# One more 384-column matmul per group, its product thrown away, in the three gather passes of a four-layer graph network

## The reference

```python
edge_index = jnp.stack([src, dst])
h = jnp.maximum(_layernorm(x, axis=-1), 0.0)
x = x + _L0_gnn_ref(h, edge_index, edge_type_9, 12500, ...)      # sum of messages by target, then a GRU cell
h = jnp.maximum(_layernorm(x, axis=-1), 0.0)
x = x + _L1_gnn_ref(h, edge_index, ...)                          # degree-scaled sum by target, matmul, norm
h = jnp.maximum(_layernorm(x, axis=-1), 0.0)
x = x + _L2_gnn_ref(h, ..., edge_index, edge_type_50)            # a matrix per relation, summed by source
h = jnp.maximum(_layernorm(x, axis=-1), 0.0)
x = x + _L3_gnn_ref(h, edge_attr_64, src, dst, ...)              # attention: softmax over each target's edges
return x
```

## Time and profile before

| | us |
|---|---|
| median of 3 runs | 12327.03 (12316.74 to 12334.25) |
| profiled execution, its own time | 12320.53 |
| its span in the trace | 12318.4 |
| layer 0 gather pass, from 303.8 to 2707 | 2403 |
| layer 1 gather pass, from 2757.6 to 5526 | 2768 |
| layer 2 message pass, from about 5550 to 8460 | 2900 |
| layer 3 soft pass, from 9216 to 11845 | 2629 |

### The profile page before, as it was taken

The page is one execution under the profiler, slowest core; times in us unless marked ns, Lnnn a source line. Parts: engine busy times, 40 slices in busy tenths (PEclk is TensorE's granted clock), DMA queues, the critical chain, the costliest instruction groups (busy, mean ns, idle before and its releaser), DMA issues. The chain is left out here.

```text
span 12318.4 us, 152974 instructions
## 1 busy us (share of the span) xinstructions
PE 8202.7 (67%) x36696; PEld 6310.6 (51%) x36696; DVE 5261.8 (43%) x13087; ACT 1875.0 (15%) x5050; POOL 7137.0 (58%) x6298
## 2 busy tenths in 40 slices
PE   0566767665565655668888888884037777777752
PEld 0455555543333333337777777773026666666641
DVE  4344444445555555552222222224424444444455
ACT  1011111111111111112222222221011111111110
POOL 0666666656555555547888888884025555555510
PEclk6555555555555555557777777776556666666655
DMA  3521121111111111114444444445512222222211
GB/s 115 208 58 56 56 58 56 56 56 53 56 56 56 56 56 56 55 54 62 56 56 55 56 56 55 56 56 107 147 53 61 60 60 59 61 59 60 60 50 33
DMA packets 891203, 798.37 MB, mean 65 GB/s; under 512 B 140837, under 2 KB 778381, under 8 KB 891132
## 3 DMA queue, kind: packets, MB, share of 16 engines
q0 software_dynamic: 376576, 415.18, 18.6%
q1 hardware_dynamic: 504956, 376.73, 9.9%
q10 hardware_dynamic: 9600, 5.66, 0.2%
HBM read 544.97 MB, written 252.04 MB: 65 GB/s over the span
## 5 line engine op out<-in xcount | busy, mean ns | idle before, releaser
L1424 POOL DMA_INDIRECT scat<-msg_out,msg_idx x1568 | 2419.2, 1543 | 497.8 <-issue 477.9
L1970 POOL DMA_INDIRECT soft_x<-proj,soft_slot x1568 | 1527.1, 974 | 1792.5 <-ACT soft_slot L1991 1319.3
L991 POOL DMA_INDIRECT L_rows<-H,L_slot x1568 | 1558.0, 994 | 1189.6 <-ACT L_slot L1006 718.9
L714 POOL DMA_INDIRECT L_rows<-H,L_slot x1568 | 1617.5, 1032 | 1059.3 <-ACT L_slot L725 600.7
L1515 PE MATMUL msg_ps_msg<-msg_hb,msg_lhs 128*128 128x128 f32 x6272 | 1599.9, 437 | 1.6 <-DVE msg_lhs L1488 1.6
L1515 PEld LDWEIGHTS msg_ps_msg<-msg_hb,msg_lhs 128*128 128x128 f32 x6272 | 1492.9, 328 | 188.9 <-issue 187.2
L1488 DVE SCALAR_TENSOR_TENSOR msg_lhs<-msg_dst_sp,msg_node,msg_ps_c 128x512 f32<-128x512 f32 x784 | 551.2, 745 | 2030.9 <-ACT msg_dst_sp L1444 2025.0
L1164 PE MATMUL L_ps_type<-L_id_rows,select 5*50 5x512 bf16 x392 | 241.1, 615 | 1027.6 <-DMA L_id_rows<-rows 546.5
L853 PE MATMUL L_sum<-L_onehot,L_rows 128*128 128x64 f32 x3136 | 714.3, 393 | 292.6 <-issue 190.6
L2037 PE MATMUL soft_ps_x<-edge_wT,soft_atT 128*128 128x256 f32 x1568 | 785.9, 600 | 99.2 <-issue 99.1
L853 PEld LDWEIGHTS L_sum<-L_onehot,L_rows 128*128 128x128 f32 x3136 | 653.1, 301 | 371.3 <-issue 269.0
(11 more groups left out here) (367 smaller groups left out, 12350.5 us busy)
## 6 DMA issues: line engine op xcount, KB each, us to landing
scat<-L_zeros SPq DMA_DIRECT2D x128, 408.0 KB
rel_parts<-scat SPq DMA_DIRECT2D x400, 128.0 KB, 2.6
L_rows<-H,L_slot POOLq DMA_INDIRECT x3136
msg_hb<-HB SPq DMA_DIRECT2D x392, 128.0 KB
soft_at_in<-in_edge_attr_dram SPq DMA_DIRECT2D x391, 128.0 KB
HB<-L_prod SPq DMA_DIRECT2D x49, 512.0 KB
scat<-msg_out,msg_idx POOLq DMA_INDIRECT x1568
soft_x<-proj,soft_slot POOLq DMA_INDIRECT x1568
```

Of the source, the lines that this page charges most:

```text
L714: pool.indirect_dma_start(rows[:, k, j, :], None, t["H0"], bass.IndirectOffsetOnAxis(ap=slot[:, k, j:j + 1], axis=0)).then_inc(gathered[k] ...
L991: pool.indirect_dma_start(rows[:, k, j, :], None, t["H1"], bass.IndirectOffsetOnAxis(ap=slot[:, k, j:j + 1], axis=0)).then_inc(gathered[k] ...
L1424: pool.indirect_dma_start(t["scat"][(k * J + j) % COPIES], bass.IndirectOffsetOnAxis(ap=idx[:, k, j:j + 1], axis=0), out[:, k, j, :], None ...
L1970: pool.indirect_dma_start(x[:, s, j, :], None, t["proj"], bass.IndirectOffsetOnAxis(ap=slot[:, s, j:j + 1], axis=0)).then_inc(gathered[s % ...
```

## The change

Ahead of PE's summing matmuls in the three passes a call issues one more matmul: the identity as weights, the 384 columns of `ih_wT` as the moving operand, into the 384 columns of the group's PSUM bank that nothing reads. In layers 0 and 1 it stands between the wait on `added` and the wait on `gathered`. In layer 3 the two waits also change places, so that it stands behind `added` and ahead of `weighed`.

```diff
+def keep_busy(pe, t, ps):
+
+    pe.matmul(ps[:, 2 * W:4 * F], t["ident"][:, :], t["ih_wT"][:, :], start=True, stop=True)
...
                 pe.wait_ge(made, n * 4 + 4)
                 pe.wait_ge(added, n * 2 + 2)
+                keep_busy(pe, t, ps_sum[s % 2])
                 pe.wait_ge(gathered[q], r * (16 * J) + 16 * J)
...
                 pe.wait_ge(made, n + 1)
                 pe.wait_ge(added, n + 2)
+                keep_busy(pe, t, ps_sum[s % 2])
                 pe.wait_ge(gathered[k], r * (16 * J) + 16 * J)
...
                 n, k, q, g = i * B + s, s % 2, s // SC, s % SC
+                pe.wait_ge(added, n + B - 1)
+                keep_busy(pe, t, ps_sum[k])
                 pe.wait_ge(weighed, n + 1)
-                pe.wait_ge(added, n + B - 1)
```

## The result

| | us |
|---|---|
| changed kernel, median of 4 runs | 12445.8 (12443.29 to 12450.57) |
| kernel before beside it, median of 4 runs | 12321.89 (12312.68 to 12334.25) |
| ratio | 1.010 (95% interval 1.0083 to 1.0118) |
| profiled execution and its span | 12447.83, 12445.8 |

The account below looks back on a forecast made before the run. The prediction took PE's own pace, with what stands in line with it, to bound the passes. Layer 1's 365, layer 0's 315 and the soft pass's 275 us made 955 us more, forecast 13280 us, range 12600 to 13700.

Parts of the forecast that it names:

- What bounds the passes: All three passes: gathered rows lie ready, PE hardly waits for them, and PE's own pace sets the time.
- The term of 315 us: Layer 0: added matmul costs 0.8 us a group, between a lower bound of zero and the full price of 466 us.
- The price of one matmul: Each of 1176 added matmuls takes PE 1.28 us at the lower clock, 0.64 us at the full clock.
- Layer 1: PE instead of DVE closes the circle between them; costs 365 us, bounds 227 to 502 us.
- The split into four groups covered and four not: Layer 1: four of eight groups pay 0.58 us after 0.70 us of standing, four pay 1.28; 7.4 us a turn.
- The clock is 0.50 throughout, and I keep it there: Layer 1: the added matmul leaves PE's granted clock at 0.50.
- Soft pass: Soft pass: added matmul costs 0.7 us a group, 275 us in all, between 442 and about -100.
- The weakest term: The granted clock: a few tenths more in layer 0 or the soft pass moves the time by hundreds of us.
- Dense groups have no idle time to hide in: Soft pass: dense groups pay the full price at the mean clock, 442 us over 392 groups.
- The 72 us that the exchange of waits was to hide: Soft pass: once in seven groups the exchanged waits hide most of the matmul, 56 x 1.28 us.
- Rival C: Mostly hidden: layer 0 0 us, soft pass +50, layer 1 227 to 365; about 12600 to 12950 us; chance 0.17.
- Rival D: Faster through granted clocks above 0.72 in layer 0 and 0.74 in the soft pass; 11800 to 12150 us; chance 0.08.

Follow-up runs that it names:

- l1_half: Kernel before plus, in layer 1 alone, one added matmul of 192 columns and five rows per group; 11274.13 us, ratio 1.0185.
- five_rows: Changed kernel with the added 384-column matmul cut to five of the 128 rows in all three passes; 12688.52 us, ratio 1.0295 to the kernel before.
- l1_five_rows: Kernel before plus the added 384-column matmul with five rows in layer 1 alone; 12708.04 us, ratio 1.0231.
- swap_only: Kernel before with only the two waits ahead of the soft pass's sums exchanged, no added matmul; 12417.61 us, ratio 1.0001.
- soft_only: Kernel before plus the added full-row matmul and the exchange of waits in the soft pass alone; 12303.93 us, ratio 0.999.
- l0_only: Kernel before plus the added full-row matmul in layer 0 alone; 12334.48 us, ratio 1.0011.
- l1_only: Kernel before plus the added full-row matmul in layer 1 alone; 12450.96 us, ratio 1.0104.
- soft_two: Kernel before plus two 384-column matmuls with full rows per group in the soft pass alone; 11114.51 us, ratio 1.0026.

## Why the prediction was wrong

**What bounds the passes: failed for layer 0, and in part for the soft pass.** "So the rows lie ready, and PE's own pace, with what stands in line with it, sets the passes" was the step that cost most. That PE didn't wait for rows was right on the chip of the result (7.4 us after the change); on the chips of the second and fourth set it does in layer 0 (508.3 us in l1_half). It didn't follow that more PE work makes the pass longer: of PE's 775 us of idle time in layer 0 the first 450 took the whole price (five_rows), although most of it had no named releaser. I had named the reason myself (the slow stretches might catch up), put the lower bound at zero, and then took 315 us, "because the idle time that has a named releaser is short". The room was the idle time, named or not. The term of 315 us measured 17.

**The price of one matmul: right.** 1.28 us more in the dense group, by the rows above. All 1176 ran (x784 in each pass is two instructions each).

**Layer 1: mechanism right, size off twice.** PE closes the circle, rows aren't waited for, the loss is there (123 of 127 us). At a clock of 0.50 it is 277 and 289 us, not 365: above the bound of 227 and below the value taken. The cover wasn't the one I counted: half of the groups at 0.70 us is 137 us, and l1_half used up the whole standing for dup, 106 us on its chip, with a matmul half as long. The rest came from other waits. PE's idle time fell by 326 us in five_rows, part of it the waits for ids (289 us there, 546.5 in the earlier trace rows), and by 317 us in l1_five_rows, where the waits for ids didn't fall; which of them takes how much isn't separated. The split into four groups covered and four not isn't shown, and l1_half, 203 us where it gives 125, speaks against it. Then "The clock is 0.50 throughout, and I keep it there" failed: it rose to 0.54, which gave back 150 and 100 us in the two sets and left 123.

**Soft pass: failed in size and sign.** The dense step of 7.0 us came as forecast, at the lower level. The step that failed is the size of what the clock gives back, "The weakest term" of the prediction: the clock went from 0.62 to 0.73, and PE's other work took 430 us less, nearly the 469 of the matmul, where 167 (442 - 275) had been allowed for everything that takes from the price. With five rows, at 0.68, 73 us remained, so here the clock matters. "Dense groups have no idle time to hide in" was read from one stretch of 20.5 us: the whole pass had 577 us of idle time, and in five_rows 185 of them went. The 72 us that the exchange of waits was to hide couldn't have been there: all idle time before L2082 was 31.0 us in the earlier trace rows. No run has the matmul without the exchange, so its share isn't measured; swap_only has nothing to hide.

**Rival C** described layer 0 and the soft pass best (0 and +50 us, measured 17 and -13), but kept the clock of layer 1, so that its range began 154 us too high. (Its own terms, 0 + 50 + 227 to 365, end at 12740, not 12950.) **Rival D's** levels, 0.72 and 0.74, were nearly reached (0.70, 0.73), with the passes close to no change as its sum says. But its reason doesn't hold in layer 0, where the clock was not needed. On the fourth chip the soft pass got 0.99 and was no shorter: the floor that D drew from POOL, 1960 us, was real, and was 1994 us there without the call (1550 and 444) and 2057 with two.

**What the clock brought.** The Trainium skill, TensorE: Matmul & The Clock Gate, section "Why this matters for your kernels", advises to keep TensorE busy for the sake of its clock. What the runs say is narrower. The clock rose with every full-row matmul of 384 columns (0.57 to 0.70, 0.50 to 0.54, 0.62 to 0.73), hardly or less with five rows (0.58, 0.50, 0.68). Only the soft pass ever got shorter with it, and not where it stood at 0.99. The most is the soft pass of soft_only: 2588 us at 0.75, against 2631 and 2639 at 0.62 in l0_only and l1_only. But that profiled execution (12261 us) is the fastest of 11 and 43 us below their median, and its layer 0, which is as before, is 16 us short too (2384 us); by the medians the kernel gained 12 us, 0.1%.

**Open.** What feeds PE so slowly in the slow stretches on some chips isn't known. The kernel before is 11 to 12% slower on those chips; that the stretches are all of it isn't shown. Whether the gathers or these stretches set layer 0 there wasn't tested: both runs meant for it fell on chips without them. POOL waits 646 us for slots in the soft pass of the changed kernel and 328 in its layer 0, where chips without the stretches have 35 and 71 us; that speaks for the stretches.

No version that computes the same beat the kernel before by more than 0.2%; the nearest is soft_only, 0.999 (0.9981 to 0.9999).

## What to carry to other kernels

Before adding work to an engine, count all of its idle time in that pass, not only the part with a named releaser: that is the most that it may take for nothing, until a run fills it. In these passes a higher TensorE clock was worth time only where TensorE was what others waited for. Look at the gathering engine's busy time plus its gaps first, since a pass lasts at least that long (2057 of 2102 us in soft_two). To price a thing in a pass where the clock answers to it, run it once in a form that leaves the clock alone: here five rows in place of 128 showed 277 us where the sum of price and clock showed 123.

## What was not expected of the hardware

Filler matmuls alone took the granted clock of a pass from 0.70 to 0.99, with PE's busy time unchanged (1875 and 1882 us). With the same 384 columns and the same pass length, layer 0 was granted 0.58 with five rows and 0.70 with 128. More busy time didn't go with more clock there (2094 against 1706 us, though a lower clock makes busy time longer by itself). It isn't that five rows never come with a rise: the soft pass went from 0.70 to 0.79 with them on the fourth chip. And the same kernel takes 11070 us on one chip and 12417 on another, at granted clocks that differ little in layer 1 (0.50 in both): the difference there, 2391 against 2782 us, is PE's idle time (750 against 1141 us).
